# Last layer, first pass over the edges: one product of the vectors moved from VectorE to ScalarE, and the edge weights of four tiles made at once

## The reference, cut to what matters

```python
def _cg_tp(s, v, y0, y1, w_ss, w_sv, w_vs, w_vv0, w_vv1):
    out_s = concatenate([w_ss * s * y0[:, None], w_vv0 * (einsum('eci,ei->ec', v, y1) / SQRT3)])
    out_v = concatenate([(w_sv * s)[:, :, None] * y1[:, None, :],
                         w_vs[..., None] * v * y0[:, None, None],
                         w_vv1[..., None] * (cross(v, y1[:, None, :]) / SQRT2)])
...
w1 = rbf @ W_rbf                              # 224 weights of an edge, from 16 numbers
m1_s, m1_v = _cg_tp(msg_s, msg_v, y0, y1, w1[...])      # first product
val_s, val_v = m1_s @ Ws_val, m1_v @ Wv_val
val_v = val_v * sigmoid(val_s @ Wg)[..., None]
val_s = sigmoid(val_s)
m2_s, m2_v = _cg_tp(val_s, val_v, y0, y1, w2_ss, ...)   # second product
h = (m2_s @ Ws_vlin, m2_v @ Wv_vlin)          # one row of 160 per edge
```

## Time and profile before

| | |
|---|---|
| median of 3 runs | 7532.61 us (7515.13 to 7553.23) |
| the profiled execution | 7540.86 us |
| its span in the trace | 7539.1 us |
| busy over the span: PE, DVE, ACT, POOL | 91%, 83%, 50%, 62% |
| the last layer's first pass, in the trace | about 4831 to 6959 us |

### The profile page before, as it was taken

One profiled execution on the slowest core, in us unless ns is written; L12 is line 12 of the kernel. 1 busy time (PEld: TensorE's weight loads), 2 busy tenths in 40 slices (PEclk: granted clock), 3 DMA queues, 4 the chain that ended last, 5 costly groups with the idle time before them and its releaser, 6 DMA issues. The chain is left out here.

```text
span 7539.1 us, 114096 instructions
## 1 busy us (share of the span) xinstructions
PE 6856.3 (91%) x33212; PEld 4573.4 (61%) x33212; DVE 6220.2 (83%) x17049; ACT 3780.0 (50%) x10162; POOL 4659.6 (62%) x3462
## 2 busy tenths in 40 slices
PE   6999999997899999989999998599999999999488
PEld 3454454545454454454444545488888888888376
DVE  6999999986677777757777777599999999998884
ACT  3555555543233222232322333377777777777485
POOL 2888888872566666526666662477777777775000
PEclk7999999996889999879999998799999999999697
DMA  8999999996222222212222220344444444444263
GB/s 226 177 178 176 175 178 175 177 170 161 57 55 56 55 56 57 49 29 58 59 57 60 58 59 23 88 97 97 95 99 96 98 97 97 98 96 87 86 189 90
DMA packets 549605, 770.78 MB, mean 102 GB/s; under 512 B 96449, under 2 KB 401126, under 8 KB 548742
## 3 DMA queue, kind: packets, MB, share of 16 engines
q0 software_dynamic: 317376, 413.42, 33.7%
q1 hardware_dynamic: 227382, 349.43, 15.1%
q10 hardware_dynamic: 4240, 0.64, 0.1%
HBM read 462.23 MB, written 300.92 MB: 101 GB/s over the span
## 5 line engine op out<-in xcount | busy, mean ns | idle before, releaser
L704 POOL DMA_INDIRECT fore<-node_table,src_i x1616 | 1709.1, 1058 | 963.1 <-issue 473.2
L1659 DVE TENSOR_TENSOR work<-work 128x384 f32<-128x384 f32 (+4 forms) x4885 | 1999.4, 436 | 63.0 <-DMA work<-src_sum 26.9
L814 POOL DMA_INDIRECT fore<-src_table,put_i x784 | 1359.0, 1733 | 449.1 <-ACT fore L1145 268.1
L771 POOL DMA_INDIRECT src_sum<-work,put_i x808 | 1283.3, 1588 | 401.1 <-issue 184.2
L1402 PE MATMUL bank<-work 128*128 128x384 f32 (+1 forms) x3232 | 1315.0, 555 | 97.8 <-DVE work L1659 86.6
L1402 PEld LDWEIGHTS bank<-work 128*128 128x128 f32 x3232 | 650.3, 212 | 850.1 <-issue 387.4
L973 ACT ACTIVATE work<-bank 64x512 f32<-64x512 f32 x404 | 239.0, 591 | 1788.3 <-PE bank L1369 1052.7
L1659 DVE TENSOR_TENSOR work<-work,bank 128x385 f32 (+4 forms) x2056 | 889.5, 433 | 173.9 <-remote 71.8
L1383 PE MATMUL bank<-w_fc,work 64*128 64x192 f32 x3232 | 660.6, 346 | 112.4 <-issue 81.4
L1383 PEld LDWEIGHTS bank<-w_fc,work 64*128 64x128 f32 x3232 | 536.4, 194 | 360.3 <-issue 323.0
L1354 PE MATMUL bank<-work 128*128 128x480 f32 x1616 | 746.3, 595 | 2.1 <-DVE work L1659 1.9
(11 more groups left out here) (280 smaller groups left out, 12742.3 us busy)
## 6 DMA issues: line engine op xcount, KB each, us to landing
edge_h<-work SPq DMA_DIRECT2D x196, 320.0 KB
work<-edge_h SPq DMA_DIRECT2D x196, 320.0 KB, 3.4
work<-keys SPq DMA_DIRECT2D x196, 256.0 KB
fore<-in_dst_row SPq DMA_DIRECT2D x196, 256.0 KB
fore<-node_table,src_i POOLq DMA_INDIRECT x1616
work<-in_edge_attr SPq DMA_DIRECT2D x196, 128.0 KB
src_sum<-work SPq DMA_DIRECT2D x4, 6240.0 KB, 40.7
work<-src_sum SPq DMA_DIRECT2D x100, 240.0 KB, 4.7
```

What stands on the lines that cost most here:

```text
L704: return pool.indirect_dma_start(dst, None, table, bass.IndirectOffsetOnAxis(ap=idx, axis=0), bounds_check=bound, oob_is_err=True)
L771: pool.indirect_dma_start(src_sum[t], bass.IndirectOffsetOnAxis(ap=put_i[:, e:e + 1], axis=0), E.run[:, g % 2, t * 480:(t + 1) * 480], Non ...
L814: pool.indirect_dma_start(T.rows[:, b, t, :], None, src_table, bass.IndirectOffsetOnAxis(ap=put_i[:, e:e + 1], axis=0), compute_op=ALU.add ...
L1659: return V_.tensor_tensor(o, p, q, op)
```

## The change

`m2` on VectorE loses the product of the vectors with `y0` (128x384 elements for a group). ScalarE makes it in a new stage `vectors_by_y0`, once for a group, in four instructions of 128x96 with `y0` as the scale, placed behind `by_y0` and ahead of `other_weights`. It waits for `vv_ready` (VectorE has the gated vectors), and `turn_m2` and VectorE's next overwriting of `vv` wait for its `vv_by_y0`.

`edge_w3` makes the weights of all four tiles of a group at once, in the turn in which it made the first two; `other_weights` copies the four tiles' 128 weights in one instruction, in the turn in which it copied the second two. `w3_mm` and `w3_out` count groups now.

```diff
 # ScalarE
 def weights_by_y0_3(h):
     b, at = h // 2 % 2, h % 2 * 2
-    act.wait_ge(s.w3_mm, h + 1)
+    if at == 0:
+        act.wait_ge(s.w3_mm, h // 2 + 1)
     for t in range(2):
-        act.activation(T.w[:, b, at + t, 0:96], bank[:, t, 0:96], ACT.Copy,
+        act.activation(T.w[:, b, at + t, 0:96], bank[:, t, at * 112:at * 112 + 96], ACT.Copy,
                        scale=y[:, h * 2 + t:h * 2 + t + 1, 0])

 def other_weights(h):
-    act.activation(T.w[:, b, at:at + 2, 96:224], bank[:, 0:2, 96:224], ACT.Copy).then_inc(s.w3_out, 1)
+    if h % 2 == 0:
+        return
+    act.activation(T.w[:, b, :, 96:224].rearrange("p (a t) c -> p t a c", t=2),
+                   bank[:, 0:2, 0:448].rearrange("p t (a c) -> p t a c", c=224)[:, :, :, 96:224],
+                   ACT.Copy).then_inc(s.w3_out, 1)

+def vectors_by_y0(h):
+    if h % 2:
+        return
+    g = h // 2
+    b = g % 2
+    act.wait_ge(s.vv_ready, g + 1)
+    for t in range(GROUP):
+        last = act.activation(T.f2[:, b, t, 160:352].rearrange("p (i c) -> p i c", c=64)[:, :, 0:V], T.vv[:, t], ACT.Copy,
+                              scale=y[:, g * GROUP + t:g * GROUP + t + 1, 0])
+    last.then_inc(s.vv_by_y0, 1)

 unrolled(TILES // 2, [(-3, m1_turned), (2, linear_out), (-6, weights_by_y0_3), (-3, values_out),
-                      (0, m2_turned), (-3, by_y0), (-6, other_weights), (-6, turns), (-9, dst_rows_out)])
+                      (0, m2_turned), (-3, by_y0), (-1, vectors_by_y0), (-6, other_weights), (-6, turns), (-9, dst_rows_out)])

 # TensorE
 def edge_w3(h):
-    if h:
-        pe.wait_ge(s.w3_out, h)
-    for t in range(2):
-        rows = slice(32 * t, 32 * t + 16)
-        last = nc.tensor.matmul(bank[:, t, 0:224], T.rb[rows, b, at * 64:at * 64 + P],
+    if h % 2:
+        return
+    if g:
+        pe.wait_ge(s.w3_out, g)
+    for t in range(GROUP):
+        rows, c0 = slice(32 * (t % 2), 32 * (t % 2) + 16), t // 2 * P
+        last = nc.tensor.matmul(bank[:, t % 2, t // 2 * 224:(t // 2 + 1) * 224], T.rb[rows, b, c0:c0 + P],
                                 wt["rbf"][rows], start=True, stop=True)
     last.then_inc(s.w3_mm, 1)

 def turn_m2(h):
     if h % 2 == 0:
         pe.wait_ge(s.m2_done, h // 2 + 1)
+        pe.wait_ge(s.vv_by_y0, h // 2 + 1)

 # VectorE, in m2(g)
+    if g:
+        dve.wait_ge(s.vv_by_y0, g)
     tt(vv, bc(cv[:, :, 68:100], 2, 3), bc(ys[:, :, 0:3], 3, V), ALU.mult)
 ...
-    tt(vv, vv, bc(f[:, :, 64:96], 2, 3), ALU.mult).then_inc(dve_own, c.step())
+    tt(vv, vv, bc(f[:, :, 64:96], 2, 3), ALU.mult).then_inc(s.vv_ready, 1)
 ...
     nine_products(vv, g)
-    tt(vsl[:, :, :, 0:V], vv, y0_planes(yy), ALU.mult).then_inc(dve_own, c.step())

 # SyncE: the same load of a group's 16 numbers waits for the same matmuls, counted by groups
-    sp.wait_ge(s.w3_mm, 2 * g - 2)
+    sp.wait_ge(s.w3_mm, g - 1)
```

More of the change, by code:

```diff
@@ L261, in build @@
             "rbf_in0", "rbf_in1", "w3_mm", "w3_out", "m1_done", "m1_turned", "m1_in_sbuf", "values_mm",
-            "sigmoid_out", "values_read", "values_out", "m2_done", "m2_turned", "m2_in_sbuf", "linear_mm", "linear_out",
+            "sigmoid_out", "values_read", "values_out", "vv_ready", "vv_by_y0", "m2_done", "m2_turned", "m2_in_sbuf", "linear_mm", "linear_out",
             "h_done", "h_kept0", "h_kept1",
@@ L1126, in weights_by_y0_3 @@
                     b, at = h // 2 % 2, h % 2 * 2
-                    act.wait_ge(s.w3_mm, h + 1)
+                    if at == 0:
+                        act.wait_ge(s.w3_mm, h // 2 + 1)
                     for t in range(2):
-                        act.activation(T.w[:, b, at + t, 0:96], bank[:, t, 0:96], ACT.Copy,
+                        act.activation(T.w[:, b, at + t, 0:96], bank[:, t, at * 112:at * 112 + 96], ACT.Copy,
                                        scale=y[:, h * 2 + t:h * 2 + t + 1, 0])
                 def other_weights(h):
-                    b, at = h // 2 % 2, h % 2 * 2
-                    act.activation(T.w[:, b, at:at + 2, 96:224], bank[:, 0:2, 96:224], ACT.Copy).then_inc(s.w3_out, 1)
+                    b, g = h // 2 % 2, h // 2
+                    if h % 2 == 0:
[3 more added lines that the diff above has]
+                                   ACT.Copy).then_inc(s.w3_out, 1)
                 def dst_rows_out(h):
@@ L1490, in edge_w3 @@
                 def edge_w3(h):
-                    g, b, at = h // 2, h // 2 % 2, h % 2 * 2
-                    if at == 0:
-                        pe.wait_ge(s.rbf_in1 if b else s.rbf_in0, 32 * (g // 2 + 1))
-                    if h:
-                        pe.wait_ge(s.w3_out, h)
-                    for t in range(2):
-                        rows = slice(32 * t, 32 * t + 16)
-                        last = nc.tensor.matmul(bank[:, t, 0:224], T.rb[rows, b, at * 64:at * 64 + P],
+                    g, b = h // 2, h // 2 % 2
+                    if h % 2:
+                        return
+                    pe.wait_ge(s.rbf_in1 if b else s.rbf_in0, 32 * (g // 2 + 1))
+                    if g:
[3 more added lines that the diff above has]
+                        last = nc.tensor.matmul(bank[:, t % 2, t // 2 * 224:(t // 2 + 1) * 224], T.rb[rows, b, c0:c0 + P],
                                                 wt["rbf"][rows], start=True, stop=True)
@@ L2336, in m1 @@
                     nine_products(mv, g)
-                    dve.wait_ge(s.w3_out, 2 * g + 2)
+                    dve.wait_ge(s.w3_out, g + 1)
                     def outer(v):
@@ L2371, in m2 @@
                     dve.wait_ge(s.sigmoid_out, 2 * g + 2)
-                    tt(vv, vv, bc(f[:, :, 64:96], 2, 3), ALU.mult).then_inc(dve_own, c.step())
-                    dve.wait_ge(dve_own, c.n - 1)
+                    tt(vv, vv, bc(f[:, :, 64:96], 2, 3), ALU.mult).then_inc(s.vv_ready, 1)
+                    dve.wait_ge(dve_own, c.n)
                     tt(scores, scores, cv[:, :, 64:68], ALU.add).then_inc(dve_own, c.step())
-                    dve.wait_ge(dve_own, c.n - 1)
+                    dve.wait_ge(s.vv_ready, g + 1)
                     nine_products(vv, g)
-                    tt(vsl[:, :, :, 0:V], vv, y0_planes(yy), ALU.mult).then_inc(dve_own, c.step())
-                    dve.wait_ge(dve_own, c.n - 1)
+                    dve.wait_ge(dve_own, c.n)
                     tt(f[:, :, 64:96], nine[:, :, 0, :], nine[:, :, 1, :], ALU.add).then_inc(dve_own, c.step())
@@ L2386, in _ @@
                 vv = T.vv
-                def y0_planes(yy):
-                    return bc(yy[:, :, 0:1].broadcast_to([P, GROUP, 3]), 3, V)
                 def edge_out(g):
```

## The result

The changed kernel takes 7854.5 us in the median of four runs (7810.8 to 7875.6), the kernel before 7542.9 in the same series. The ratio is 1.040, 95% interval 1.036 to 1.044: slower, as forecast, but by 312 us instead of 216. The profiled execution took 7810.8 us. The range ended at 7840; the time lies 15 us above it.

What follows compares the result with a forecast made beforehand. TensorE was taken as the bound, its loop running through ScalarE. Routes of 6.71 and 5.17 us plus 0.05 for loads gave 11.93 us a group against 10.83, 216 us over 196 groups: 7748 us, 2.9% slower, range 7650 to 7840.

Steps and rivals of the forecast that it cites:

- TensorE sets the pace, VectorE waits, ScalarE's spare time lies at one place: Whole loop: VectorE waits for ScalarE and ScalarE for TensorE; ScalarE's spare 22% lies where it must wait for `values`.
- Route A: TensorE's loop from `values` in the odd turn to `values` in the even turn: 5.17 us before, 6.71 forecast.
- route B: TensorE's loop from `values` in the even turn to the next odd turn: 5.52 us before, 5.17 forecast.
- a group 11.88: Both turns of TensorE's loop together, without register loads: 11.88 us forecast instead of 10.69.
- the way to TensorE: In Route A, from the end of ScalarE's merged copy of the weights to TensorE's next start: 0.05 us.
- the destination tile: In Route A, TensorE's work between the weights and `values` in the even turn: 0.33 us.
- 216 us for the waits: Whole pass: 1.10 us more a group, 11.93 against 10.83, over 196 groups, from TensorE's longer waits for ScalarE.
- 0.05 us a group for the loads: TensorE's register loads in every fourth odd turn: 0.22 of 0.54 us left outside the wait for copy L1123.
- The clock falls (0.07): Rival, chance 0.07: TensorE's new waits lower its clock to 0.91 in the mean, 147 us on top, 7895 us.
- No wait for `vv_ready`: ScalarE's four new instructions start right behind `by_y0`, since VectorE's product ends earlier; no wait.
- VectorE over 2 us a group: Sign in the changed profile: VectorE waits over 2 us a group, ahead of `m2` for the most part.
- GpSimd's gathers: nothing: Gathers wait for L1145, 1.2 us later in the odd turn, but run groups ahead of use: no cost.

Runs made afterwards that it cites:

- in the gap: Kernel before with only the vectors' product moved to ScalarE, placed where ScalarE waits for `values`, weights by halves: ratio 1.000 (0.996 to 1.003), pass 2128 us.

## Why the prediction was right and wrong

- *TensorE sets the pace, VectorE waits, ScalarE's spare time lies at one place.* Right, and shown twice: the vectors' product leaves VectorE without any gain (ratio 1.000 in the gap), and it costs 161 us or nothing by its place alone.
- *Route A 6.71 us, route B 5.17, a group 11.88.* Measured 6.71, 5.16 and 11.87. That this is so exact is luck. The pieces: four instructions 1.07 us instead of 0.96, the copy of the weights 0.58 instead of 0.61, the way to TensorE 0.14 instead of 0.05, the weights 0.95 instead of 1.16, the destination tile 0.38 instead of 0.33. Five errors that cancel. The step of 0.27 for a scaled ACTIVATE, worked out by the Trainium skill ("ScalarE: Activation LUTs"), was the better one: 5508.43 to 5509.50 is 0.27 each.
- *216 us for the waits.* Groups at the full clock take 11.88 us, loads of registers included, against 10.83, so the term was some 206 us; the pass without the clock's patches comes to 2334 us, where about 2340 was forecast. I had left 0.05 us a group for the loads; they vanished in TensorE's waits.
- *"The clock falls (0.07)", kept a rival because the longest standstill is about 0.9 us.* This is the step that failed, and the only one that mattered. The sum has no term for the clock. The standstill was 1.01 us and the clock fell, to 0.96 in the mean: some 80 us of the pass in the profiled execution, 88 in the next. Together with the 206 us this makes the 286 of the pass, and it is why the time left the range: with the standstill filled and the clock at 1.00 the kernel takes 7756 us, inside it. The Trainium skill's rule on the clock gate ("TensorE: Matmul & The Clock Gate"), that idleness brings the half rate back, holds here with 0.50 in the 2 us quoted. I had two grounds against it. That the present small waits, 0.47 us in every fourth group, leave the clock at 1.00 told nothing of waits twice as long, and no row said that 0.9 us is harmless. The price was too high and the chance too low: at 0.91 I had 147 us, and the rows show 0.96.
- *No wait for `vv_ready`, VectorE over 2 us a group.* Right: VectorE is idle (2415 - 2005.5) / 196 = 2.09 us a group, of this 1.28 us in front of `m2` and 113.8 us in 162 groups, 0.70 each, in front of the weights' product.
- *GpSimd's gathers: nothing.* Right for the changed kernel, whose pace is slower. For a faster one it is the next bound, at 10.9 us a group wherever the long gather comes.

## What to carry to other kernels

The share of idle time of an engine says nothing about what it can take over; read in front of which instruction it is idle, and put the new work there. An engine that is busy 50 to 80% can be on the loop that sets the pace for all but one of its places. When a change makes TensorE stand still about a microsecond in every round, count its clock too: filling the standstill with work that nobody needs made this kernel 105 us faster, some 87 of them by the clock. And before mending one slow instruction in a queue, count in the rows which one of its kind it is.

## What was not expected of the hardware

- TensorE's clock fell to the 1.2 GHz level in patches in a stage in which it was busy 89.4% and, from the third group to the last few, never idle for more than 1.02 us in one piece. Standstills of 0.80 or of 0.48 us a group left it at 1.00.
- Four matmuls of 16 rows, alternating between two groups of rows, start faster in one run: 0.95 us for eight recorded ones against 0.58 for four.
- GpSimd's gathers take mostly 1.0 to 2.0 us each, but the third by source in a group took 3.05 us in some stretches and runs when its queue ran without a break, and in others of the same kernel it did not; the cause is open.
